# A WKV recurrence rewritten as one phase: token shift inside the projections' weights, four exponents from one difference, the inverse by logarithm and a Newton step

## The chip, the cores and the metric

The kernel runs on one core of a Trainium2 chip. TensorE (PE in the profile) multiplies matrices, VectorE (DVE), ScalarE (ACT) and GpSimd (POOL) work on elements, and each engine runs its own instruction stream in order and meets the others at semaphores. The metric is the device time in microseconds of the whole program; lower is better.

## The reference

The program is a model of several layers over 2 sequences of 1024 tokens with 128 channels: attention, mixtures of experts, and one RWKV layer. The change touches the RWKV layer alone, which computes:

```
xx = concatenate([zeros_like(x[:, :1]), x[:, :-1]], axis=1)
xk = x * time_mix_k + xx * (1.0 - time_mix_k)      # the same for v and r
k, v, r = xk @ W_key.T, xv @ W_value.T, xr @ W_receptance.T
w = -exp(time_decay)
def step(carry, kv_t):                             # over tokens
    p, q, o = carry
    no = maximum(o, u + kt)
    A, Bc = exp(o - no), exp(u + kt - no)
    y = (A * p + Bc * vt) / (A * q + Bc)
    no2 = maximum(w + o, kt)
    A2, B2 = exp(w + o - no2), exp(kt - no2)
    return ((A2 * p + B2 * vt, A2 * q + B2, no2), y)
out = (sigmoid(r) * wkv) @ W_output.T
```

Here `x` is the layer-normed input, `u` is `time_first`, and the output is added to the residual.

## The kernel before

The program is a row of phases. `phase` gives each engine its own block of code, and ends with a barrier of all engines that also clears the phase's semaphores, so nothing of the next phase starts before the last engine of this one is done. Inside a phase `Chain.link` marks an instruction with a semaphore and makes the engine wait for it; `Chain.mark` only marks it.

`rwkv` keeps data with the 128 channels on the partitions and tokens along the free dimension, so one instruction on a sequence is 128x1024. It is called once in `program`, between two calls of `block_l1`. Its pieces in order:

1. `passage` adds the previous block's output to the residual, normalizes, transposes on TensorE and lets ScalarE write the normed input to `rw_x` (line 315). `rw_x` has 1025 columns per sequence, a zero and then the tokens, so the shifted input is the same buffer one column earlier.
2. A phase for constants (lines 1640 to 1653): zeros and start values, `1 - time_mix`, and `-exp(time_decay)` in `rw_w`.
3. A phase for the token shift (1656 to 1667): ScalarE scales `rw_x` by `time_mix` for k, v and r (128x2048 each), and VectorE adds the shifted input scaled by `1 - time_mix`.
4. `products`, a phase of 12 matmuls 128x512 (line 171). Two engines take turns in copying the results from PSUM, VectorE (line 191) and ScalarE (line 200); r passes a sigmoid there.
5. The recurrence's phase (1672 to 1726). VectorE finds `o` by a scan over tokens with add and max (line 1692), forms `no` and the arguments of A, Bc and A2 (1695 to 1698), GpSimd forms B2's (1677), ScalarE takes four exponents for each sequence (1726). Then VectorE scans `q` and `p` (1705, 1707), forms numerator and denominator (1708 to 1712) with GpSimd's product of Bc and v (1680), takes the reciprocal (1713), and multiplies by it and by the gate (1714, 1715). Sequence 0 runs through all of this before sequence 1 starts its second half.
6. `enter_l1`, a `passage` whose first matmuls (line 258) project the result.

The order on each engine is that of the code; there is no scheduler. An fp32 matmul shows as two records of MATMUL in the trace, so the 12 matmuls of step 4 are 24 records. A switch between functions of ScalarE for which the build needs another table puts an ACT_TABLE_LOAD ahead of the activation.

Of the kernel before, what the change touches and what calls it, by code (L numbers as in the profile page):

```python
# [1627 lines left out]
def rwkv(S, D):  # L1628
    with ExitStack() as ctx:
# [10 lines left out]
        with phase(S, 2) as (block, (done, to_act)):  # L1640
            @block.vector
            def _(dve):
                dve.memset(Xs[:, :, 0:1], 0.0)
# [7 lines left out]
            @block.scalar
            def _(act):
                act.activation(wdec[:], S.tdecay[:], ACT.Exp).then_inc(to_act, 1)

        mixes = (mix, A, Bc)
        with phase(S, 1) as (block, (scaled,)):
            @block.scalar
            def _(act):
                for i in range(3):
# [2 lines left out]
            @block.vector
            def _(dve):
                for i in range(3):
                    dve.wait_ge(scaled, i + 1)
                    out = split_b(mixes[i])
                    dve.scalar_tensor_tensor(out, Xs[:, :, 0:T], om[:, i:i + 1], out, ALU.mult, ALU.add)
# [202 lines left out]
```

## Time and profile before

| | |
|---|---|
| time, median of 3 runs (lowest to highest) | 2785.84 us (2783.7 to 2789.19) |
| profiled execution: its time, its span | 2787.93 us, 2786.2 us |
| granted TensorE clock, mean over the span | 0.882 |
| busy: PE, DVE, ACT, POOL | 80%, 57%, 52%, 29% |
| stretch from the end of the first `passage` to the first matmul of `enter_l1` | 2188.7 to 2278.3 us, 89.6 us |
| in that stretch busy: PE, DVE, ACT, POOL | 12.85, 70.91, 22.60, 11.64 us |

The page's shares are over the whole span, in which the RWKV layer is a small part. The stretch of interest is cut out by its times, and its rows are read in order of time. Times in the trace count from the start of the span; the 1.7 us between span and time lie outside of it.

### The profile page before, as it was taken

What the parts mean: (1) busy time and instruction counts of PE and PEld (TensorE: products, weight loads), DVE (VectorE), ACT (ScalarE), POOL (GpSimd) and SP (SyncE); (2) the same over time, 40 slices, a digit from 0 to 9 for tenths busy, and PEclk for the clock granted to TensorE, in tenths of its full rate; (3) what the DMA queues carried; (4) which work ended last, traced back from release to release, by engine and by line L of the source; (5) the groups of instructions that cost most, each with busy time, mean ns of one, the idle gap of its engine ahead of it and who ended that gap; (6) DMA issues with size and microseconds to landing.
All of it is one profiled execution on the core that took longest, in us unless ns stands there. A gap on an engine that the chain in (4) does not pass through costs nothing. (4 is left out here: it accounts for less than half of the span.)

```text
span 2786.2 us, 37366 instructions
## 1 busy us (share of the span) xinstructions
PE 2224.0 (80%) x13838; PEld 1285.9 (46%) x13838; DVE 1588.6 (57%) x3402; ACT 1437.1 (52%) x2136; POOL 804.1 (29%) x384
## 2 busy tenths in 40 slices
PE   4999999999999718499619485999979425999888
PEld 2656666666666415333315243344347212444357
DVE  4777777776776445411355444777433685777324
ACT  2666676666766351388542243455642312555541
POOL 2677777776776201322001203100000022000000
PEclk8899999999999858699759696899989656999999
DMA  2000000000000130321310312211010002210000
GB/s 71 8 1 1 3 8 1 3 8 1 1 3 1 53 103 1 81 67 35 100 56 1 93 33 56 61 36 36 2 31 1 1 0 70 64 36 19 1 31 16
DMA packets 41660, 82.91 MB, mean 30 GB/s; under 512 B 10744, under 2 KB 18472, under 8 KB 37320
## 3 DMA queue, kind: packets, MB, share of 16 engines
q1 hardware_dynamic: 41480, 80.52, 10.7%
q8 instruction: 112, 1.84, 0.3%
q14 instruction: 68, 0.56, 0.1%
HBM read 66.11 MB, written 13.63 MB: 29 GB/s over the span
## 5 line engine op out<-in xcount | busy, mean ns | idle before, releaser
L685 ACT ACTIVATE probs<-psum_banks 128x1024 f32<-128x1024 f32 (+3 forms) x608 | 474.3, 826 | 367.2 <-PE psum_banks L550 260.0
L1096 POOL TENSOR_SCALAR l0a_rows<-l0a_rows,l0a_rinv 128x1024 f32<-128x1024 f32 x192 | 562.2, 2935 | 253.5 <-DVE l0a_rinv L1074 253.3
L758 DVE TENSOR_REDUCE neg_max<-psum_banks 128x1 f32<-128x512 f32 (+3 forms) x672 | 398.8, 658 | 201.4 <-PE psum_banks L583 149.7
L1062 DVE TENSOR_REDUCE l0a_nmax<-psum_banks 128x1 f32<-128x1024 f32 x256 | 312.9, 1222 | 208.7 <-PE psum_banks L955 208.0
L545 PE MATMUL psum_banks<-q_stack,k_stack 75*128 75x512 bf16 (+7 forms) x1216 | 324.9, 345 | 74.5 <-ACT probs L685 25.6
L1009 ACT ACTIVATE l0a_rows<-psum_banks,l0a_nmax 128x1024 f32<-128x1024 f32 x256 | 285.9, 1117 | 81.8 <-DVE l0a_nmax L1062 79.3
L579 PE MATMUL psum_banks<-k_stack,q_stack 72*128 72x128 bf16 (+3 forms) x1024 | 250.3, 328 | 78.1 <-DMA q_stack<-q_parts 66.5
L969 PE MATMUL psum_banks<-packed,l0a_rows 128*128 128x128 f32 x2048 | 267.7, 274 | 7.8 <-POOL l0a_rows L1096 6.3
L954 PE MATMUL psum_banks<-l0a_kh,l0a_qw 128*128 128x512 f32 x512 | 257.4, 503 | 6.1 <-DVE l0a_qw L1030 5.8
L969 PEld LDWEIGHTS psum_banks<-packed,l0a_rows 128*128 128x128 f32 x2048 | 237.9, 141 | 52.5 <-POOL l0a_rows L1096 11.5
L567 PE MATMUL psum_banks<-probs,v_ones 128*32 128x512 f32 (+3 forms) x2432 | 245.8, 520 | 7.5 <-ACT o_sum L654 6.5
L545 PEld LDWEIGHTS psum_banks<-q_stack,k_stack 75*128 75x128 bf16 (+1 forms) x1216 | 106.5, 101 | 254.6 <-ACT probs L685 104.5
L955 PE MATMUL psum_banks<-l0a_kl,l0a_qw 128*128 128x512 f32 x512 | 205.8, 402 | 0.0
L579 PEld LDWEIGHTS psum_banks<-k_stack,q_stack 72*128 72x128 bf16 x1024 | 95.3, 105 | 201.8 <-DVE neg_max L758 90.3
L954 PEld LDWEIGHTS psum_banks<-l0a_kh,l0a_qw 128*128 128x128 f32 x512 | 97.8, 191 | 134.6 <-issue 79.0
L1004 ACT ACTIVATE x_norm<-psum_banks 128x512 f32<-128x512 f32 x128 | 75.9, 593 | 136.8 <-PE psum_banks L969 136.7
L1677 POOL TENSOR_TENSOR rw_b<-rw_k,rw_o 128x1024 f32<-128x1024 f32 x2 | 4.0, 1998 | 459.2 <-DVE rw_o L1692 459.2
L550 PE MATMUL psum_banks<-tri_k,ident_b 128*128 128x128 bf16 (+1 forms) x576 | 133.8, 249 | 0.0
L1623 DVE SCALAR_TENSOR_TENSOR l1f_y<-psum_banks,rt_g,l1f_y 128x128 f32<-128x128 f32 x256 | 72.1, 344 | 103.5 <-PE psum_banks L1561 103.5
L1585 ACT ACTIVATE l1f_h<-psum_banks 128x512 f32<-128x512 f32 x128 | 75.7, 599 | 105.5 <-PE psum_banks L1547 105.2
L981 PE MATMUL psum_banks<-x_norm,l0a_v 128*64 128x512 f32 x512 | 124.0, 604 | 3.7 <-ACT l0a_ot L1014 3.7
L1547 PE MATMUL psum_banks<-x_norm_t,l1f_w 128*128 128x512 f32 x256 | 115.7, 610 | 12.4 <-DMA l1f_w<-in_l1f_w 10.8
(270 smaller groups left out, 3420.9 us busy)
## 6 DMA issues: line engine op xcount, KB each, us to landing
q_stack<-q_parts SPq DMA_DIRECT2D x96, 192.0 KB
k_stack<-k_parts SPq DMA_DIRECT2D x72, 192.0 KB
qkv<-in_l0f_w SPq DMA_DIRECT2D x6, 1024.0 KB, 5.3
q_parts<-parts SPq DMA_DIRECT2D x24, 256.0 KB
k_parts<-parts SPq DMA_DIRECT2D x24, 256.0 KB
moe_b<-in_l0f_b SPq DMA_DIRECT2D x32, 128.0 KB, 4.7
l1f_w<-in_l1f_w SPq DMA_DIRECT2D x16, 256.0 KB, 4.9
moe_w<-in_l0f_w SPq DMA_DIRECT2D x2, 1024.0 KB, 5.5
```

The lines of the kernel that those rows point to most:

```text
L545: m = pe.matmul(PS[:, bank, c0:HALF], S.Kst[0:rows_of_stack, slot(g, i), kt * P:(kt + 1) * P], S.Qst[0:rows_of_stack, slot(g, i), side * H ...
L550: m = pe.matmul(PS[:, bank, c0:c1], S.ident_b[:], S.tri_k[:, 0:c1 - c0], start=False, stop=True, skip_group_check=True)
L567: m = pe.matmul(PS[32 * i:32 * (i + 1), 7, c0:HALF], S.Vx[:, NT * b + kt, h0 + i, :], S.Pt[:, U % PBUFS, i, c0:HALF], start=kt == 0, stop= ...
L579: return pe.matmul(bank[:, at:at + k1 - k0], S.Qst[0:72, slot(g, i), jq * P:(jq + 1) * P], S.Kst[0:72, slot(g, i), k0:k1], start=first, st ...
L685: act.activation(S.Pt[:, U % PBUFS, 2 * half:2 * half + 2, c0:HALF], PS[:, bank:bank + 2, c0:HALF], ACT.Exp).then_inc(exp_done, 1)
L758: dve.tensor_reduce(out, scores, AX, ALU.max, negate=True).then_inc(job_read, 1)
L954: pe.matmul(scores(s)[:, c0:c0 + HALF], q, R.Kh[:, b, c0:c0 + HALF], start=True, stop=False)
L955: m = pe.matmul(scores(s)[:, c0:c0 + HALF], q, R.Kl[:, b, c0:c0 + HALF], start=False, stop=True)
L969: m = pe.transpose(PS[:, 4 + a, jj * P:(jj + 1) * P], R.Pr[:, (NT * ps + 2 * jj + a) % RING, kt * P:(kt + 1) * P], S.ident[:])
L1009: act.activation(R.Pr[:, s % RING, :], scores(s), ACT.Exp, bias=R.nmax4[:, s % 4:s % 4 + 1], accum_out=R.rsum4[:, s % 4:s % 4 + 1]).then_i ...
L1062: dve.tensor_reduce(R.nmax4[:, s % 4:s % 4 + 1], scores(s), AX, ALU.max, negate=True).then_inc(max_done, 1)
L1096: pool.tensor_scalar(R.Pr[:, s % RING, :], R.Pr[:, s % RING, :], R.rinv4[:, s % 4:s % 4 + 1], None, ALU.mult).then_inc(pool_normed, 1)
```

## The change

The phases 2 to 5 become one phase with 14 semaphores.

- The shift goes into the weights. For each of k, v and r two scaled copies of the weight are made (`rw_scaled`, 128x128 each): weight times `time_mix` and weight times `1 - time_mix`. Each bank of 512 tokens is the sum of two matmuls, on `rw_x` and on `rw_x` one column earlier. These are 24 matmuls in place of 12.
- k, v and r stay in PSUM: banks 0 to 3 hold k and later r, banks 4 to 7 hold v. The copies of lines 191 and 200 are gone, VectorE reads k and v from PSUM, and ScalarE reads r for the sigmoid.
- With Z = k - o(previous), all four exponents are `exp(-relu(...))` of Z or -Z with a bias for each channel. VectorE does one scan and one subtraction for a sequence; ScalarE does four Relu and four Exp.
- The reciprocal (1713) is replaced by Ln, Exp of the negative on ScalarE, and a Newton step of three instructions on VectorE that also multiplies the numerator in. GpSimd does nothing in this phase: its subtraction (1677) is gone with the arguments, and its product of Bc and v (1680) moves to VectorE.
- Both sequences' second halves run before either one's division.

```diff
-        mix = S.sb("rw_mix", [P, N])
-        K, V, R = (S.sb(f"rw_{x}", [P, N]) for x in "kvr")
...
+        Z, A, Bc, A2, B2 = (S.sb(f"rw_{x}", [P, B, T]) for x in ("z", "a", "bc", "a2", "b2"))
+        num, den, inv, gate, out = (S.sb(f"rw_{x}", [P, B, T]) for x in ("num", "den", "inv", "gate", "out"))
+        scaled, rest = S.sb("rw_scaled", [P, 3, 2, P]), S.sb("rw_rest", [P, 3])
+        decay, neg_decay, neg_first = (S.sb(f"rw_{x}", [P, 1]) for x in ("decay", "neg_decay", "neg_first"))
...
+        def banks(first, b):
+            return S.PS[:, first + 2 * b:first + 2 * b + 2, :].rearrange("p a c -> p (a c)")
...
+        with phase(S, 14) as (block, (dve_done, act_done, primed, decayed, k_scaled, vr_scaled, k_ready, v_ready, r_ready, z_ready,
+                                      exp_out, den_ready, inverse, gated)):
...
+                def project(i, first, b):
+                    for n in range(T // HALF):
+                        for j in range(2):
+                            t0 = n * HALF + 1 - j
+                            m = pe.matmul(S.PS[:, first + 2 * b + n, :], scaled[:, i, j, :], Xs[:, b, t0:t0 + HALF],
+                                          start=j == 0, stop=j == 1)
+                    return m
+
+                pe.wait_ge(primed, 1)
+                pe.wait_ge(k_scaled, 2)
+                for b in range(B):
+                    project(0, 0, b).then_inc(k_ready, 1)
+                pe.wait_ge(vr_scaled, 4)
+                for b in range(B):
+                    project(1, 4, b).then_inc(v_ready, 1)
+                for b in range(B):
+                    pe.wait_ge(z_ready, b + 1)
+                    project(2, 0, b).then_inc(r_ready, 1)
...
+                ch.link(dve.tensor_scalar(rest[:], S.tmix[:], -1.0, 1.0, ALU.mult, ALU.add))
+                for j, share in enumerate((S.tmix, rest)):
+                    dve.tensor_scalar(scaled[:, 0, j, :], weights[0], share[:, 0:1], None, ALU.mult).then_inc(k_scaled, 1)
...
+                dve.memset(Xs[:, :, 0:1], 0.0).then_inc(primed, 1)
+                dve.wait_ge(primed, 1)
+                dve.wait_ge(decayed, 1)
+                for b in range(B):
+                    dve.wait_ge(k_ready, b + 1)
+                    ch.link(dve.tensor_tensor_scan(O[:, b, cur], decay[:].to_broadcast([P, T]), banks(0, b), -1e38, ALU.add, ALU.max))
+                    dve.tensor_tensor(Z[:, b], banks(0, b), O[:, b, prev], ALU.subtract).then_inc(z_ready, 1)
+                for b in range(B):
+                    dve.wait_ge(exp_out, 4 * b + 2)
+                    ch.mark(dve.tensor_tensor_scan(Qn[:, b, cur], A2[:, b], B2[:, b], 0.0, ALU.mult, ALU.add))
+                    dve.wait_ge(v_ready, b + 1)
+                    ch.link(dve.tensor_tensor(B2[:, b], B2[:, b], banks(4, b), ALU.mult))
+                    dve.wait_ge(exp_out, 4 * b + 4)
+                    ch.link(dve.tensor_tensor(den[:, b], Qn[:, b, prev], A[:, b], ALU.mult))
+                    dve.tensor_tensor(den[:, b], den[:, b], Bc[:, b], ALU.add).then_inc(den_ready, 1)
+                    ch.mark(dve.tensor_tensor(Z[:, b], Bc[:, b], banks(4, b), ALU.mult))
+                    ch.link(dve.tensor_tensor_scan(Pn[:, b, cur], A2[:, b], B2[:, b], 0.0, ALU.mult, ALU.add))
+                    ch.link(dve.tensor_tensor(num[:, b], Pn[:, b, prev], A[:, b], ALU.mult))
+                    ch.mark(dve.tensor_tensor(num[:, b], num[:, b], Z[:, b], ALU.add))
+                for b in range(B):
+                    dve.wait_ge(inverse, b + 1)
+                    dve.wait_ge(den_ready, b + 1)
+                    ch.link(dve.tensor_tensor(B2[:, b], den[:, b], inv[:, b], ALU.mult))
+                    ch.link(dve.scalar_tensor_tensor(inv[:, b], B2[:, b], 2.0, inv[:, b], ALU.subtract, ALU.mult))
+                    ch.link(dve.scalar_tensor_tensor(num[:, b], num[:, b], -1.0, inv[:, b], ALU.mult, ALU.mult))
+                    dve.wait_ge(gated, b + 1)
+                    dve.tensor_tensor(out[:, b], num[:, b], gate[:, b], ALU.mult)
...
-                    act.activation(split_b(mixes[i]), Xs[:, :, 1:T1], ACT.Copy, scale=S.tmix[:, i:i + 1]).then_inc(scaled, 1)
...
+                a = Chain(act, act_done)
+                a.link(act.activation(neg_decay[:], S.tdecay[:], ACT.Exp))
+                act.activation(decay[:], neg_decay[:], ACT.Copy, scale=-1.0).then_inc(decayed, 1)
+                a.mark(act.activation(neg_first[:], S.tfirst[:], ACT.Copy, scale=-1.0))
+                act.wait_ge(dve_done, 1)
+                for i in (1, 2):
+                    for j, share in enumerate((S.tmix, rest)):
+                        act.activation(scaled[:, i, j, :], weights[i], ACT.Copy, scale=share[:, i:i + 1]).then_inc(vr_scaled, 1)
...
+                    act.wait_ge(z_ready, b + 1)
+                    four = (A2, 1.0, neg_decay[:]), (B2, -1.0, decay[:]), (A, 1.0, S.tfirst[:]), (Bc, -1.0, neg_first[:])
+                    for x, sign, bias in four:
+                        a.mark(act.activation(x[:, b], Z[:, b], ACT.Relu, bias=bias, scale=sign))
+                    a.wait()
+                    for x, _, _ in four:
+                        act.activation(x[:, b], x[:, b], ACT.Exp, scale=-1.0).then_inc(exp_out, 1)
...
+                    act.wait_ge(den_ready, b + 1)
+                    a.link(act.activation(inv[:, b], den[:, b], ACT.Ln))
+                    act.activation(inv[:, b], inv[:, b], ACT.Exp, scale=-1.0).then_inc(inverse, 1)
+                    if b == 0:
+                        for c in range(B):
+                            act.wait_ge(r_ready, c + 1)
+                            act.activation(gate[:, c], banks(0, c), ACT.Sigmoid).then_inc(gated, 1)
...
-                for b in range(B):
-                    pool.wait_ge(scanned, b + 1)
-                    pool.tensor_tensor(split_b(B2)[:, b, :], split_b(K)[:, b, :], O[:, b, 1:T1], ALU.subtract).then_inc(b2_in, 1)
...
-                    ch.link(dve.reciprocal(a2, a2))
-                    ch.link(dve.tensor_tensor(k, k, a2, ALU.mult))
-                    ch.link(dve.tensor_tensor(k, k, r, ALU.mult))
```

The instructions of one sequence on VectorE, between exponents and gate. Before, from the scan of `rw_qn` to the product with the gate `rw_r` (`SCALAR_TENSOR_TENSOR` at lines 1705 and 1707 is the scan; buffer numbers are left out, so `rw_a` is A or A2 and `rw_b` is B2):

```order
L1705 SCALAR_TENSOR_TENSOR rw_qn<-rw_a,rw_b 128x1024
L1706 TENSOR_TENSOR rw_k<-rw_b,rw_v 128x1024
L1707 SCALAR_TENSOR_TENSOR rw_pn<-rw_a,rw_k 128x1024
L1708 TENSOR_TENSOR rw_k<-rw_pn,rw_a 128x1024
L1709 TENSOR_TENSOR rw_a<-rw_qn,rw_a 128x1024
L1711 TENSOR_TENSOR rw_k<-rw_k,rw_x 128x1024
L1712 TENSOR_TENSOR rw_a<-rw_a,rw_bc 128x1024
L1713 RECIPROCAL rw_a<-rw_a 128x1024
L1714 TENSOR_TENSOR rw_k<-rw_k,rw_a 128x1024
L1715 TENSOR_TENSOR rw_k<-rw_k,rw_r 128x1024
```

Of the change, the second sequence's part at the same place and the first sequence's division right behind it:

```order
L1689 SCALAR_TENSOR_TENSOR rw_qn<-rw_a,rw_b 128x1024
L1691 TENSOR_TENSOR rw_b<-rw_b,psum_banks 128x1024
L1693 TENSOR_TENSOR rw_den<-rw_qn,rw_a 128x1024
L1694 TENSOR_TENSOR rw_den<-rw_den,rw_bc 128x1024
L1695 TENSOR_TENSOR rw_z<-rw_bc,psum_banks 128x1024
L1696 SCALAR_TENSOR_TENSOR rw_pn<-rw_a,rw_b 128x1024
L1697 TENSOR_TENSOR rw_num<-rw_pn,rw_a 128x1024
L1698 TENSOR_TENSOR rw_num<-rw_num,rw_z 128x1024
L1702 TENSOR_TENSOR rw_b<-rw_den,rw_inv 128x1024
L1703 SCALAR_TENSOR_TENSOR rw_inv<-rw_b,rw_inv 128x1024
L1704 SCALAR_TENSOR_TENSOR rw_num<-rw_num,rw_inv 128x1024
L1706 TENSOR_TENSOR rw_out<-rw_num,rw_gate 128x1024
```

Ten instructions for a sequence become twelve; the reciprocal is gone, and one product with v came from GpSimd (`rw_z`).

ScalarE at the end of the phase. Before, the last rows of the phase are the sigmoids of step 4 and the exponents:

```order
L200 ACT_TABLE_LOAD
L200 ACTIVATE rw_r<-psum_banks 128x512 x4
L66 UNCONDITIONAL_BRANCH
L1717 UNCONDITIONAL_BRANCH
L1726 ACT_TABLE_LOAD
L1726 ACTIVATE rw_a<-rw_a 128x1024
```

Of the change, from the last exponent of the second sequence to the last inverse:

```order
L1727 ACTIVATE rw_bc<-rw_bc 128x1024
L1730 ACT_TABLE_LOAD
L1730 ACTIVATE rw_inv<-rw_den 128x1024
L1731 ACT_TABLE_LOAD
L1731 ACTIVATE rw_inv<-rw_inv 128x1024
L1735 ACT_TABLE_LOAD
L1735 ACTIVATE rw_gate<-psum_banks 128x1024 x2
L1730 ACT_TABLE_LOAD
L1730 ACTIVATE rw_inv<-rw_den 128x1024
L1731 ACT_TABLE_LOAD
L1731 ACTIVATE rw_inv<-rw_inv 128x1024
```

The sigmoids moved from in front of the exponents to between the two sequences' inverses, and five table loads stand in this tail.

## Rows read from the trace of the kernel before

**Rows 1.** Page, part 1: busy time and share of each engine.

```profile
PE 2224.0 (80%) x13838; PEld 1285.9 (46%) x13838; DVE 1588.6 (57%) x3402; ACT 1437.1 (52%) x2136; POOL 804.1 (29%) x384
```

**Rows 2.** Windows: length, busy PE, PEld, DVE, ACT, POOL, granted clock, DMA.

```profile
2188.70:2278.30 89.60, 12.85 (x24) 5.40 (x24) 70.91 (x43) 22.60 (x25) 11.64 (x4) 0.56 0.00 0
2188.70:2201.70 13.00, 0.00 (x0) 0.00 (x0) 7.29 (x9) 7.29 (x6) 0.00 (x0) 0.50 0.00 1
...
2236.00:2278.30 42.30, 0.00 (x0) 0.00 (x0) 40.93 (x21) 2.01 (x3) 4.36 (x1) 0.50 0.00 0
```

**Rows 3.** Timeline, from the passage's end to the last projection.

```profile
2188.11 0.60 ACT L315 ACTIVATE rw_x<-psum_banks 128x512 f32<-128x512 f32 x1 [0.64 <-PE psum_banks L268]
...
2189.82 0.06 DVE L1643 MEMSET rw_x<- 128x2 f32 x1 [2.98 <-PEq L69]
...
2201.73 5.98 PE L171 MATMUL psum_banks<-rw_mix,packed 128*128 128x512 f32 x8 [13.66 <-PEq L69]
...
2203.81 0.69 DVE L191 COPY rw_k<-psum_banks 128x512 f32<-128x512 f32 x1 [2.79 <-PE psum_banks L171]
...
2207.55 3.60 PE L171 MATMUL psum_banks<-rw_a,packed 128*128 128x512 f32 x8
...
2207.75 0.60 ACT L200 ACTIVATE rw_k<-psum_banks 128x512 f32<-128x512 f32 x1 [1.64 <-PE psum_banks L171]
```

**Rows 4.** Windows again: the granted clock (third number from the end).

```profile
2180.00:2190.00 10.00, 3.36 (x13) 2.15 (x12) 6.75 (x38) 2.83 (x7) 0.00 (x0) 0.50 0.00 0
...
2201.00:2206.00 5.00, 4.27 (x5) 1.85 (x6) 0.72 (x2) 0.48 (x1) 0.00 (x0) 0.50 0.01 2
...
2208.00:2212.00 4.00, 4.00 (x11) 1.85 (x10) 1.39 (x2) 1.74 (x4) 0.00 (x0) 1.00 0.00 0
```

**Rows 5.** Timeline of the recurrence: first scan, second half, end.

```profile
2215.93 2.29 DVE L1692 TENSOR_TENSOR_SCAN rw_o<-rw_w,rw_k 128x1024 f32<-128x1024 f32 x1 [4.91 <-PEq L69]
...
2222.56 1.28 DVE L1697 SCALAR_TENSOR_TENSOR rw_bc<-rw_k,packed,rw_mix 128x1024 f32<-128x1024 f32 x1
2222.68 1.06 ACT L1726 ACTIVATE rw_a<-rw_a 128x1024 f32<-128x1024 f32 x1 [5.50 <-DVE rw_a L1696]
...
2235.99 2.28 DVE L1705 TENSOR_TENSOR_SCAN rw_qn<-rw_a,rw_b 128x1024 f32<-128x1024 f32 x1
2236.04 4.36 POOL L1680 TENSOR_TENSOR rw_x<-rw_v,rw_bc 128x1024 f32<-128x1024 f32 x1 [3.45 <-ACT rw_bc L1726]
...
2238.19 3.29 DVE L1706 TENSOR_TENSOR rw_k<-rw_b,rw_v 128x1024 f32<-128x1024 f32 x1
...
2259.95 1.20 DVE L1706 TENSOR_TENSOR rw_k<-rw_b,rw_v 128x1024 f32<-128x1024 f32 x1
...
2268.30 6.55 DVE L1713 RECIPROCAL rw_a<-rw_a 128x1024 f32<-128x1024 f32 x1
2274.89 1.23 DVE L1714 TENSOR_TENSOR rw_k<-rw_k,rw_a 128x1024 f32<-128x1024 f32 x1
2276.15 1.23 DVE L1715 TENSOR_TENSOR rw_k<-rw_k,rw_r 128x1024 f32<-128x1024 f32 x1
...
2278.33 4.42 PE L258 MATMUL psum_banks<-packed,rw_k 128*128 128x128 f32 x24 [63.75 <-PEq L69]
```

**Rows 6.** Groups by line, whole span: count, busy us, mean ns.

```profile
L1018 ACT ACTIVATE l0a_rows<-l0a_rows,l0a_rinv 128x1024 f32<-128x1024 f32 x64 | 73.2, 1143 | 0.0
...
L354 DVE TENSOR_SCALAR x_norm<-l1f_y,ln_mv,ln_rstd 128x128 f32<-128x128 f32 x32 | 8.9, 343 | 0.3
```

**Rows 7.** Timeline of ScalarE around a switch of table, 2211 to 2216 us.

```profile
2211.18 0.60 ACT L200 ACTIVATE rw_v<-psum_banks 128x512 f32<-128x512 f32 x1 [1.12 <-PE psum_banks L171]
...
2211.80 1.28 ACT L200 ACT_TABLE_LOAD   x1
...
2213.09 2.12 ACT L200 ACTIVATE rw_r<-psum_banks 128x512 f32<-128x512 f32 x4
```

More of the change, by code:

```diff
@@ new lines, in rwkv @@
+        num, den, inv, gate, out = (S.sb(f"rw_{x}", [P, B, T]) for x in ("num", "den", "inv", "gate", "out"))
+        scaled, rest = S.sb("rw_scaled", [P, 3, 2, P]), S.sb("rw_rest", [P, 3])
+        decay, neg_decay, neg_first = (S.sb(f"rw_{x}", [P, 1]) for x in ("decay", "neg_decay", "neg_first"))
+        weights = [S.w["rwkv"][x] for x in "kvr"]
+        passage(S, S.X, add=S.Y, to=lambda g: Xs[:, g // 2, 1 + g % 2 * HALF:1 + (g % 2 + 1) * HALF])
+        prev, cur = slice(0, T), slice(1, T1)
@@ L1641, in _ @@
             @block.vector
             def _(dve):
-                dve.memset(Xs[:, :, 0:1], 0.0)
+                ch = Chain(dve, dve_done)
+                ch.link(dve.tensor_scalar(rest[:], S.tmix[:], -1.0, 1.0, ALU.mult, ALU.add))
+                for j, share in enumerate((S.tmix, rest)):
+                    dve.tensor_scalar(scaled[:, 0, j, :], weights[0], share[:, 0:1], None, ALU.mult).then_inc(k_scaled, 1)
                 dve.memset(O[:, :, 0:1], -1e38)
@@ L1646, in _ @@
                 dve.memset(Qn[:, :, 0:1], 0.0)
-                dve.tensor_scalar(om[:], S.tmix[:], -1.0, 1.0, ALU.mult, ALU.add)
-                dve.wait_ge(to_act, 1)
-                dve.tensor_scalar(wdec[:], wdec[:], -1.0, None, ALU.mult)
+                dve.memset(Xs[:, :, 0:1], 0.0).then_inc(primed, 1)
[5 more added lines that the diff above has]
+                    dve.tensor_tensor(Z[:, b], banks(0, b), O[:, b, prev], ALU.subtract).then_inc(z_ready, 1)
@@ L1651, in _ @@
             @block.scalar
             def _(act):
[L1653 to L1659, printed above, removed]
-                    act.activation(split_b(mixes[i]), Xs[:, :, 1:T1], ACT.Copy, scale=S.tmix[:, i:i + 1]).then_inc(scaled, 1)
[L1662 to L1667, printed above, removed]
@@ new lines, in _ @@
+                a.wait()
+                act.wait_ge(decayed, 1)
+                for b in range(B):
+                    act.wait_ge(z_ready, b + 1)
+                    four = (A2, 1.0, neg_decay[:]), (B2, -1.0, decay[:]), (A, 1.0, S.tfirst[:]), (Bc, -1.0, neg_first[:])
+                    for x, sign, bias in four:
+                        a.mark(act.activation(x[:, b], Z[:, b], ACT.Relu, bias=bias, scale=sign))
+                    a.wait()
+                    for x, _, _ in four:
+                        act.activation(x[:, b], x[:, b], ACT.Exp, scale=-1.0).then_inc(exp_out, 1)
@@ new lines, in _ @@
+                for b in range(B):
+                    act.wait_ge(den_ready, b + 1)
[5 more added lines that the diff above has]
+                            act.activation(gate[:, c], banks(0, c), ACT.Sigmoid).then_inc(gated, 1)
+        enter_l1(S, None, token_units(S, S.w["rwkv"]["o"], S.X, src=out.rearrange("p b t -> p (b t)"), add_scale=1.0))
```

54 lines of the change are left out of this document (2 added, 52 removed).

## The prediction

> **What bounds the kernel now.** I read the page's first part only to see that it doesn't decide: over the whole span TensorE is busy 80% and VectorE 57% [rows 1], but the change touches one stretch, and the barriers on both sides of it keep anything from moving in or out. So the second view is the windows of that stretch. From 2188.7 to 2278.3 us VectorE is busy 70.9 of 89.6 us, ScalarE 22.6, TensorE 12.9 [rows 2]. The reader should see two kinds of time in it. In the first 13.0 us TensorE does nothing, while the shift is computed for the whole input before any matmul. In the last 42.3 us VectorE is busy for 40.9 and the others hardly at all [rows 2]. The timeline then gives the borders, and I take four pieces from it:
>
> - head, from VectorE's first memset at 2189.82 to the first projection at 2201.73 [rows 3];
> - projections, from there to the first scan at 2215.93 [rows 3, 5];
> - arguments and exponents, from there to the scan of q at 2235.99, 20.06 us [rows 5];
> - second half, from there to the end of the last product, 2276.15 + 1.23 = 2277.38, 41.39 us [rows 5].
>
> VectorE is the bound in the last two, and the order of phases in the first two. Any microsecond taken off this chain comes off the time, because every later phase starts at a barrier.
>
> **The change on the same clock.** I lay out the new phase from the same first instant, 2189.82. Durations at 128x1024: an operation on two tensors 1.23, a scan 2.29, one with a pointer scalar 1.28 [rows 5]. A linked successor starts 0.03 behind the end (2274.89 + 1.23 to 2276.15); one that doesn't wait overlaps its predecessor by 0.08 (2235.99 + 2.28 against 2238.19) [rows 5]. So linked operations cost 1.26, 1.31 and 2.32 us, unlinked ones 1.15 and 2.20.
>
> *Head.* VectorE makes `rest`, two scaled weights of 0.34 each [rows 6] and four memsets (0.06) [rows 3]. With overlaps that is about 1.0 us, so TensorE starts at 2190.8 instead of 2201.73: **10.9 us** gained. ScalarE meanwhile makes constants and the four scaled weights for v and r; they have until k is projected, some 9 us, and are hidden.
>
> *Projections.* Twice as many matmuls, but only k's first four stand ahead of the first scan. The clock was at 0.50, the 1.2 GHz level, while the passage's short transposes ran (2180 to 2190), still at 0.50 from 2201 to 2206 with TensorE working, and at 1.00, the 2.4 GHz level, from 2208 on [rows 4]. Before, the fourth matmul's result reached ScalarE at 2207.75, 6.02 us behind the start, and the next four (eight records) took 2210.98 - 2207.55, which is 3.43 at full clock (the row's 3.60 holds the last one's overhang) [rows 3]. I assume the same warm-up. k is there at 2196.8 for sequence 0 and 2200.25 for sequence 1; v at 2203.7 and 2207.1; r at 2210.5 and 2214. The first scan starts 6.0 us behind the projections' start instead of 14.2: **8.2 us**. This also removes three barriers. Where no row fits is the scan that reads PSUM. Nothing excludes that it costs as little as a scan from SBUF, 2.29; above, the slowest wide VectorE operation here is the reciprocal with 6.55 [rows 5]. I take 2.29, since a copy of 512 columns from PSUM (0.69 [rows 3]) is far nearer to a scan's pace than to the reciprocal's, and keep 6.55 for the range.
>
> *Arguments and exponents.* Scan 2196.82 to 2199.11, Z until 2200.4. ScalarE then does four Relu with a bias pointer. The nearest row is an activation with a pointer, 1.14, against 1.06 without [rows 5, 6]; successive ones overlap by about 0.1 (four sigmoids of 0.60 take 2.12 [rows 7]). Four Relu 4.3 us, then two exponents 2.0: the scan of q starts at 2206.8, against 9.98 us behind the first scan instead of 20.06: **10.1 us**. Sequence 1's scan and Z (2200.3 to 2203.8) lie in VectorE's wait for these exponents. Here ScalarE, not VectorE, ends the wait: VectorE idles for about 3 us.
>
> *Second half.* For each sequence: scan 2.20, `rw_b` times v 1.26, denominator 1.26 + 1.15, product of Bc and v 1.15, scan 2.32, numerator 1.26 + 1.15 (the 1.15s are those that nothing directly behind waits for). That is 11.75, twice 23.5, to 2230.3. Then the division and gate: 1.26 + 1.31 + 1.31 + 1.15 = 5.03, twice 10.1, ending at 2240.4 or 2240.5. So 33.7 us instead of 41.4: **7.7 us**. Check by parts: two reciprocals (2 x 6.58) go, and the contention of line 1706's first instance, which took 3.29 beside a GpSimd product of 4.36 and 1.20 alone [rows 5], goes with GpSimd: 15.2 less. The division and gate come to 5.03 instead of 2.5 for a sequence, and Bc times v is 1.15: 7.4 more. The difference, 7.8, agrees.
>
> *ScalarE's tail, costed at nothing.* After sequence 1's exponents (about 2216.9): load, Ln, load, Exp for sequence 0 (to 2221.7), load and two gates (to 2224.9), load, Ln, load, Exp for sequence 1 (to 2229.7), with 1.28 for a load and 1.06 for an activation [rows 5, 7]. VectorE asks for the first inverse at 2230.3 and for the second at 2235.4. What hides this work is VectorE's second half; the slack is 8.6 and 5.7 us. Without that cover it would cost all its 12.8 us. TensorE's r is 10 us early for the gates.
>
> *End barrier.* A barrier clears the phase's semaphores. Behind the passage (15) it took 1.1 us (2188.11 + 0.60 to 2189.82) [rows 3], behind the recurrence (6) 0.95 (2277.38 to 2278.33) [rows 5]. With 14 I add 0.15.
>
> Sum: 10.9 + 8.2 + 10.1 + 7.7 - 0.15 = 36.75, I say **36.8 us**. On the profiled execution's own time, 2787.93, that is 2751.1, with a span of 2749.4; that execution lay 2.1 us above the median of the runs, inside their spread. Against the median 2785.84 it is **2749 us**.
>
> **A rule weighed against a row.** When ScalarE switched tables at 2211.8, the load began 0.02 us behind the last activation's end and the sigmoid began 1.29 us later [rows 7]; so I price a switch at 1.29. The Trainium skill (ScalarE: Activation LUTs, section What ACT_TABLE_LOAD costs) puts a drain of 1.38 us on top, 2.66 in all. By it the five switches of the tail would cost 6.9 us more, the second inverse would come at 2236.5 and be 1.1 us late, and the sum would be 35.7 instead of 36.8. The trace speaks against the rule as far as a visible gap goes.
>
> **The rivals.**
>
> 1. *TensorE stays at 1.2 GHz through the phase.* For it: 0.50 over the whole passage and up to 2206 [rows 4]. Against: it rose within some 5 us of steady work. Then k comes 1.2 and 4.6 us later, v at 2211.7 and 2218.5, r at 2225.4 and 2232.2; VectorE waits for v, and the second inverse, behind both gates on ScalarE, comes at 2238. End at 2243.2, 2.7 later: 2751.7.
> 2. *TensorE is at 2.4 GHz at once,* as it idles only 2.7 us before. The first four matmuls take 3.8 instead of 6.0: 2746.8. Against it: 0.50 with intermittent work directly before [rows 4].
> 3. *The scan from PSUM goes at the reciprocal's pace,* 6.55. Both first scans grow by 4.3, of which 5.9 show once the wait for the exponents has taken its share: 2754.9.
> 4. *ScalarE's tail becomes the bound.* If each of the five switches took twice its row, 6.4 us more, the second inverse would be 0.7 late: 2749.7. It decides from 1.15 a switch. Beside it stands the skill's rule above, with 2750.1.
> 5. *The other side, slower: wide VectorE operations contend with ScalarE as they did with GpSimd.* Line 1706 took 3.29 us beside GpSimd and 1.20 alone [rows 5]. The new phase keeps both engines on SBUF and PSUM at once for most of its length. At 3.25 instead of 1.23 for each of the 22 wide operations that are no scans the loss is 44.4, more than the gain by 7.6: 2793. It decides from 19 of the 22. Against it: line 1697, from 2222.56, ran in 1.28 while ScalarE took an exponent from 2222.68, and the scan of 2235.99 wasn't stretched even beside GpSimd (2.28) [rows 5].
> 6. *The change saves here and the rest gives it back,* through a lower granted clock in the 508 us behind it. Nothing in the rows does that; it would end within 0.2%.
>
> **How the numbers follow.** Forecast 0.76; rivals 0.07, 0.05, 0.04, 0.04, 0.02, 0.02 in that order. The likeliest gives 2749. Single runs before lay 2.1 below to 3.4 above their median. The range starts about 3.5 below rival 2 and ends 2 above rival 3: 2743 to 2757. A measurement of this kernel tells about 0.2%, 5.6 us, from no change. All cases but the last two are faster by 31 to 39 us: faster 0.97, same 0.01, slower 0.02 (of rival 6 half is counted as same, half, where only a part is given back, as faster).
>
> **What would show it.** In the changed profile: first projection 1.0 us behind the first VectorE instruction; first scan some 6 us later, in 2.3 us; four Relu of 1.14 and Exps of 1.06 ahead of the scan of q; VectorE without a gap over 0.1 us from there to the end, 33.7 us; no wait for `rw_inv` or `rw_gate`; the stretch 52.8 us instead of 89.6; what lies ahead and behind within a microsecond or two of before. Wrong if the PSUM-reading operations are longer than their SBUF kin, if VectorE's rows are stretched beside ScalarE, if a wait for an inverse shows, or if the 508 us behind change their length.

## The result and the profile after

The changed kernel takes 2750.12 us (median of 4 runs, 2749.71 to 2750.74), beside 2787.52 us before (4 runs, 2783.7 to 2789.27). The ratio is 0.9868, with a 95% interval of 0.9851 to 0.9885: 37.4 us less in the medians, where 36.8 us and a time of 2749 us were forecast.

The timeline of VectorE in the changed kernel, from the constants to the first matmul of `enter_l1` (which stands in TensorE's own timeline, last row; columns as in [rows 3]):

```profile
2186.57 0.17 DVE L1674 TENSOR_SCALAR rw_rest<-packed 128x3 f32<-128x3 f32 x1 [2.94 <-PEq L69]
...
2193.88 2.29 DVE L1685 TENSOR_TENSOR_SCAN rw_o<-rw_decay,psum_banks 128x1024 f32<-128x1024 f32 x1 [6.58 <-PE psum_banks L1656]
2196.20 1.22 DVE L1686 TENSOR_TENSOR rw_z<-psum_banks,rw_o 128x1024 f32<-128x1024 f32 x1
...
2203.88 2.29 DVE L1689 TENSOR_TENSOR_SCAN rw_qn<-rw_a,rw_b 128x1024 f32<-128x1024 f32 x1 [3.00 <-ACT rw_b L1727]
2206.09 1.19 DVE L1691 TENSOR_TENSOR rw_b<-rw_b,psum_banks 128x1024 f32<-128x1024 f32 x1
...
2227.26 1.22 DVE L1702 TENSOR_TENSOR rw_b<-rw_den,rw_inv 128x1024 f32<-128x1024 f32 x1
2228.51 1.22 DVE L1703 SCALAR_TENSOR_TENSOR rw_inv<-rw_b,rw_inv 128x1024 f32<-128x1024 f32 x1
...
2232.17 1.22 DVE L1702 TENSOR_TENSOR rw_b<-rw_den,rw_inv 128x1024 f32<-128x1024 f32 x1
...
2235.94 1.23 DVE L1706 TENSOR_TENSOR rw_out<-rw_num,rw_gate 128x1024 f32<-128x1024 f32 x1
```

```profile
2187.41 23.50 PE L1656 MATMUL psum_banks<-rw_x,rw_scaled 128*128 128x512 f32 x48 [2.55 <-DVE rw_x L1680]
2237.94 5.46 PE L258 MATMUL psum_banks<-packed,rw_out 128*128 128x128 f32 x24 [27.03 <-PEq L69]
```

Inside the phase only two rows of VectorE carry a wait: 6.58 us for k, and 3.00 us for the exponent of B2 (the 2.94 us of the first row are the barrier behind the passage). Behind 2203.88 there is none up to the last product, where the kernel before had its reciprocals and a product of 3.29 us [rows 5].

I call the distance from VectorE's first instruction behind the passage to the first matmul of line 258 the stretch: 88.51 us before (2189.82 to 2278.33 [rows 3, 5]), 51.37 us now (2186.57 to 2237.94), 37.14 less. (The prediction's 52.8 us count from the end of the passage's last row instead, 2184.90 + 0.60 in the changed kernel; by that count it is 52.44.) By the prediction's pieces:

| piece | before | forecast | measured | gain |
|---|---|---|---|---|
| head, to the first projection | 11.91 | 1.0 | 0.84 | 11.07 |
| projections, to the first scan | 14.20 | 6.0 | 6.47 | 7.73 |
| arguments and exponents, to the scan of q | 20.06 | 9.98 | 10.00 | 10.06 |
| second half, to the end of the last product | 41.39 | 33.7 | 33.29 | 8.10 |
| barrier, to the next matmul | 0.95 | 1.10 | 0.77 | 0.18 |

ScalarE's tail in the changed kernel's timeline:

```profile
2212.78 1.04 ACT L1727 ACTIVATE rw_bc<-rw_bc 128x1024 f32<-128x1024 f32 x1
2213.84 1.28 ACT L1730 ACT_TABLE_LOAD   x1
2215.14 1.06 ACT L1730 ACTIVATE rw_inv<-rw_den 128x1024 f32<-128x1024 f32 x1
2216.21 1.28 ACT L1731 ACT_TABLE_LOAD   x1
2217.50 1.06 ACT L1731 ACTIVATE rw_inv<-rw_inv 128x1024 f32<-128x1024 f32 x1
2218.58 1.28 ACT L1735 ACT_TABLE_LOAD   x1
2219.87 1.94 ACT L1735 ACTIVATE rw_gate<-psum_banks 128x1024 f32<-128x1024 f32 x2
2221.83 1.28 ACT L1730 ACT_TABLE_LOAD   x1
...
2225.49 1.06 ACT L1731 ACTIVATE rw_inv<-rw_inv 128x1024 f32<-128x1024 f32 x1
```

The first inverse is there at 2218.56 and asked for at 2227.26, the second at 2226.55 and asked for at 2232.17. Each of the five switches takes 1.30 to 1.32 us from the end of one activation to the start of the next.

The span fell by 38.0 us (2786.2 to 2748.2), 0.9 more than the stretch. Ahead of the stretch the changed execution is 3.25 us shorter (2189.82 against 2186.57), behind it 2.39 longer (507.87 against 510.26), with the same code on both sides. Such differences come in every run below. The part behind the stretch took 506.15 us in e2_old_args and 513.75 in e6_div_at_once, with the same 2873 matmul records. The windows of that part in these two, columns as in [rows 2]:

```profile
2248.25:2754.40 506.15, 423.55 (x2873) 233.45 (x2873) 277.28 (x721) 230.13 (x319) 30.75 (x24) 0.90 0.13 33
```

```profile
2246.05:2759.80 513.75, 431.26 (x2873) 235.63 (x2873) 277.32 (x721) 230.31 (x319) 30.74 (x24) 0.88 0.13 32
```

TensorE is busy 7.7 us longer in the second, at a granted clock of 0.88 instead of 0.90, while VectorE's busy time is the same. So the whole time can't tell edits of 2 or 3 us apart here, and the experiments are read by the stretch first.

### The profile page after: what moved, and what is told of

Its sections match the earlier page's. It is cut to its first block and busy times, and to the rows that moved or that the text cites. A ratio compares the mean times of both kernels' runs of the same rounds, so it can differ in the third digit from the quotient of the medians.

```text
span 2748.2 us, 37340 instructions
## 1 busy us (share of the span) xinstructions
PE 2231.7 (81%) x13852; PEld 1292.2 (47%) x13862; DVE 1558.0 (57%) x3394; ACT 1445.4 (53%) x2148; POOL 792.4 (29%) x380
## 5 line engine op out<-in xcount | busy, mean ns | idle before, releaser
L371 POOL TENSOR_SCALAR l1f_y<-x_res,ln_mv,ln_rstd 128x128 f32<-128x128 f32 x32 | 25.9, 819 | 569.3 <-DVE ln_rstd L351 569.3
L550 PE MATMUL psum_banks<-tri_k,ident_b 128*128 128x128 bf16 (+1 forms) x566 | 127.5, 243 | 0.0
```

Of the source, the lines that this page charges most:

```text
L550: m = pe.matmul(PS[:, bank, c0:c1], S.ident_b[:], S.tri_k[:, 0:c1 - c0], start=False, stop=True, skip_group_check=True)
```

## The experiments

The kernel before, run beside them, took 2786.03 us (19 runs, first four experiments), 2782.17 (7 runs, next four) and 2784.29 (9 runs, last four). My theory: the gain is the sum of four things taken off VectorE's chain, each worth what its rows say, and ScalarE's longer tail costs nothing while VectorE's second half covers it. The main rival: the work has only moved, and ScalarE or TensorE is waited for in its place.

**e1_recip: the reciprocal again.**

```diff
-                    dve.wait_ge(inverse, b + 1)
...
-                    ch.link(dve.tensor_tensor(B2[:, b], den[:, b], inv[:, b], ALU.mult))
-                    ch.link(dve.scalar_tensor_tensor(inv[:, b], B2[:, b], 2.0, inv[:, b], ALU.subtract, ALU.mult))
-                    ch.link(dve.scalar_tensor_tensor(num[:, b], num[:, b], -1.0, inv[:, b], ALU.mult, ALU.mult))
+                    ch.link(dve.reciprocal(inv[:, b], den[:, b]))
+                    ch.link(dve.tensor_tensor(num[:, b], num[:, b], inv[:, b], ALU.mult))
```

> The changed kernel with VectorE's reciprocal in place of Ln, Exp and the Newton step; ScalarE keeps only the two gates in its tail. Stretch here and below: from VectorE's first instruction behind the passage to the first matmul of line 258, 88.5 us before and 51.4 changed. Theory (the inverse by logarithm is worth what it takes off VectorE): a sequence's end goes from 4.91 to 6.58 + 1.26 + 1.15 = 8.99 us, so 8.1 more in all: stretch 59.5, time 8 us over the changed kernel's 2750.1, 2758. Rival (ScalarE's tail is waited for anyway, so the division is no net gain): stretch within 1 us of 51.4.

Measured: stretch 59.59 us (2190.20 to 2249.79), 8.2 more than the changed kernel's; time 2760.52 us, 10.4 more than its 2750.12. From e1_recip's timeline, the end of one sequence:

```profile
2230.97 6.55 DVE L1701 RECIPROCAL rw_inv<-rw_den 128x1024 f32<-128x1024 f32 x1
2237.55 1.23 DVE L1702 TENSOR_TENSOR rw_num<-rw_num,rw_inv 128x1024 f32<-128x1024 f32 x1
2238.81 1.22 DVE L1704 TENSOR_TENSOR rw_out<-rw_num,rw_gate 128x1024 f32<-128x1024 f32 x1
2239.95 6.54 DVE L1701 RECIPROCAL rw_inv<-rw_den 128x1024 f32<-128x1024 f32 x1
```

8.98 us from reciprocal to reciprocal where the change takes 4.91 (2227.26 to 2232.17). The logarithm's route is worth 8.2 us, all of it through ScalarE doing its part in VectorE's shadow.

**e2_old_args: the four arguments on VectorE again.**

```diff
-                    dve.tensor_tensor(Z[:, b], banks(0, b), O[:, b, prev], ALU.subtract).then_inc(z_ready, 1)
+                    dve.scalar_tensor_tensor(A2[:, b], O[:, b, prev], decay[:], O[:, b, cur], ALU.add, ALU.subtract).then_inc(inverse, 1)
+                    dve.tensor_tensor(B2[:, b], banks(0, b), O[:, b, cur], ALU.subtract).then_inc(inverse, 1)
+                    ch.link(dve.scalar_tensor_tensor(num[:, b], banks(0, b), u, O[:, b, prev], ALU.add, ALU.max))
...
-                        a.mark(act.activation(x[:, b], Z[:, b], ACT.Relu, bias=bias, scale=sign))
```

> The changed kernel with the four arguments formed on VectorE as in the kernel before (five instructions behind each scan in place of one) and no Relu on ScalarE. Theory (VectorE's arguments are the chain and there is nothing that they could hide behind but the 3.0 us wait): per sequence 8.3 us from scan to scan instead of 3.5; the scan of q starts 16.6 us behind the first scan instead of 10.0, stretch 51.4 + 6.6 = 58.0, time 2757. The wait of 3.0 us for the exponents is gone. Rival (the work is only moved to ScalarE, whose four Relu are waited for just as long): stretch 51 to 53.

Measured: stretch 56.85 us, 5.5 more; time 2759.03 us, 8.9 more. From the first scan (2197.60) to the scan of q (2214.20) it is 16.6 us, as expected, without a wait. The stretch is 1.1 us less than expected because k came 5.36 us behind the first projection instead of 6.47; that varies from run to run (below). At the changed kernel's 6.47 it would be 57.96.

**e3_shift_alone: the kernel before with the shift in the weights.**

```diff
-                    dve.scalar_tensor_tensor(out, Xs[:, :, 0:T], om[:, i:i + 1], out, ALU.mult, ALU.add)
...
+        products(S, [Unit([(slice(0, HALF), [(scaled[:, i, j, :], Xs[:, n // 2, n % 2 * HALF + 1 - j:(n % 2 + 1) * HALF + 1 - j])
+                                             for j in range(2)])],
+                          dst[:, n * HALF:(n + 1) * HALF], func=ACT.Sigmoid if i == 2 else None)
+                     for i, dst in enumerate((K, V, R)) for n in range(N // HALF)])
```

> The kernel before with one part alone: the shift inside the weights, as 24 matmuls in place of 12 within the old phase of projections, all ahead of the recurrence. Theory (this part pays only because in the changed kernel just four matmuls stand ahead of the first scan): TensorE starts 2.3 us behind VectorE's first instruction instead of 11.9, 9.5 less, and its phase is 24 records of 0.43 longer, 10.3 more: stretch 88.5 + 0.8 = 89.3, no change in time that can be told. Rival (saving the elementwise shift is the gain of head and projections): stretch about 79, time 9 us less than before.

Measured: stretch 88.91 us (2190.44 to 2279.35), 0.4 longer; time 2788.55 us, ratio to before 1.0012 (1.0003 to 1.0022). TensorE started 2.33 us behind VectorE's first instruction, and its 48 records took 22.8 us. The rival is out: saving the elementwise shift, without a change of the order, gains nothing. What is left for the 18.8 us that head and projections gained is the order: only k's first four matmuls stand in front of the first scan, no barrier stands between, and nothing is copied out of PSUM. No run takes these apart, and none has the new order with the elementwise shift. Rows of the kernel before tell what that would cost:

```profile
2192.11 2.00 ACT L1660 ACTIVATE rw_mix<-rw_x,packed 128x2048 f32<-128x2048 f32 x1 [0.87 <-PEq L69]
...
2194.15 2.35 DVE L1667 SCALAR_TENSOR_TENSOR rw_mix<-rw_x,rw_om,rw_mix 128x2048 f32<-128x2048 f32 x1 [2.72 <-ACT rw_mix L1660]
...
2205.52 0.60 ACT L200 ACTIVATE rw_k<-psum_banks 128x512 f32<-128x512 f32 x1 [7.62 <-PE psum_banks L171]
```

Mixing k alone takes 4.4 us (2192.11 to 2196.50), and its first two matmuls 3.8 (2201.73 to 2205.52): 8.2 us to the first scan, where the changed kernel needs 7.3 (2186.57 to 2193.88). By this estimate the shift in the weights would be worth only about 1 us of the 18.8, if VectorE's additions for v and r (2.35 us each) fit into its waits.

**e4_no_pool: the kernel before without GpSimd in the recurrence.**

```diff
-                    pool.tensor_tensor(Xs[:, b, 0:T], split_b(V)[:, b, :], split_b(Bc)[:, b, :], ALU.mult).then_inc(weighted, 1)
...
+                    dve.tensor_tensor(b2, k, O[:, b, cur], ALU.subtract).then_inc(b2_in, 1)
...
+                    ch.link(dve.tensor_tensor(Xs[:, b, 0:T], v, bc, ALU.mult))
```

> The kernel before with GpSimd's four operations in the recurrence done by VectorE. Theory (VectorE's long rows beside GpSimd are contention): lines 1695, 1696 and 1706 all take 1.2 to 1.3 us instead of up to 3.3, which is 7.8 us less, and four more operations of 1.15 are 4.6 more: stretch 85.3, 3.2 less, 0.1% of the time. Rival (they are long for another reason, their operands or the first use of a buffer): the rows stay above 3 us and the stretch grows by 4.6 to 93.1.

Measured: stretch 85.19 us, 3.3 less; time 2787.25 us, ratio 1.0005 (0.9994 to 1.0017), so the whole time doesn't show it. The timelines do. Before, beside GpSimd, three rows of VectorE took 3.1 to 3.3 us besides line 1706's [rows 5]; two of them:

```profile
2218.26 3.12 DVE L1695 SCALAR_TENSOR_TENSOR rw_mix<-rw_k,packed,rw_o 128x1024 f32<-128x1024 f32 x1
...
2230.43 3.25 DVE L1696 TENSOR_TENSOR rw_a<-rw_o,rw_mix 128x1024 f32<-128x1024 f32 x1
```

The same instructions, and line 1706's, in e4_no_pool:

```profile
2215.95 1.28 DVE L1686 SCALAR_TENSOR_TENSOR rw_mix<-rw_k,packed,rw_o 128x1024 f32<-128x1024 f32 x1
...
2225.58 1.22 DVE L1687 TENSOR_TENSOR rw_a<-rw_o,rw_mix 128x1024 f32<-128x1024 f32 x1
...
2232.45 1.20 DVE L1698 TENSOR_TENSOR rw_k<-rw_b,rw_v 128x1024 f32<-128x1024 f32 x1
```

GpSimd made VectorE's four rows longer by 7.8 us (two of 3.12, one of 3.25, one of 3.29) and saved it 4.5. The kernel before shows how [rows 5]: a scan starts at 2235.99, GpSimd's product 0.05 us later and takes 4.36, and VectorE's next product takes 3.29 and ends 1.1 us behind it. The Trainium skill (SBUF — State Buffer, section SBUF: two separate sides) says that VectorE, when it reads two inputs from SBUF, and GpSimd share a port pair, and that whichever starts first holds it for its whole instruction. The trace agrees: 4.36 is near 2.28 for the scan plus the 2.00 that GpSimd's subtraction of the same size takes (line 1677), and the 1.1 us that VectorE's product still needs once GpSimd is done is near the 1.20 that it takes alone.

**e5_pairs: ScalarE does A2 and B2 first.**

```diff
-                    for x, sign, bias in four:
-                        a.mark(act.activation(x[:, b], Z[:, b], ACT.Relu, bias=bias, scale=sign))
-                    a.wait()
...
+                    for two in (four[:2], four[2:]):
+                        for x, sign, bias in two:
+                            a.mark(act.activation(x[:, b], Z[:, b], ACT.Relu, bias=bias, scale=sign))
+                        a.wait()
```

> The changed kernel with ScalarE's order per sequence changed: Relu and Exp of A2 and B2 first, then Relu and Exp of A and Bc. Theory (VectorE's only wait inside the recurrence, 3.0 us for the exponent of B2, holds two Relu that it doesn't need): the scan of q starts two Relu, 2.1 us, earlier, the stretch is 49.4 instead of 51.4 us; A and Bc come 8.3 us behind Z, still ahead of their use. Rival (the wait moves to the second pair, since the denominator needs A and Bc): a new wait of 1 to 2 us in front of line 1693 takes it back, stretch 51.

Measured: stretch 49.00 us, of which 1.1 is an early k (5.39 us). Both sides were right in part. From e5_pairs' waits (who waited for whom, us in total, times, longest):

```profile
DVE rw_qn L1689 <- ACT rw_b L1728: 0.9, 1, 0.9
DVE rw_den L1693 <- ACT rw_bc L1728: 0.8, 1, 0.8
```

The wait of 3.0 us is 0.9 now, and a new one of 0.8 stands in front of the denominator. From first scan to last product it is 41.97 us instead of 43.29: 1.3 gained. The time doesn't show it: 2756.46 us is 6.3 more than the changed kernel's, and 0.9900 of the kernel before run beside it (0.9883 to 0.9917) where the change had 0.9868. The profiled execution spends 513.67 us behind its stretch, the changed kernel's 510.26, with the same code. So the gain is shown for the stretch alone.

**e6_div_at_once: the cover taken away.**

```diff
-                for b in range(B):
                     dve.wait_ge(inverse, b + 1)
```

(the division goes into the loop of the second halves, directly behind each numerator)

> The changed kernel with each sequence's division right behind its numerator, as in the kernel before, so VectorE's second half of sequence 1 no longer covers ScalarE's Ln and Exp of sequence 0. Theory: the first inverse can't be ready before ScalarE has done the exponents of sequence 1 and four pieces of 1.07 to 1.29 us, 14.7 us behind the start of the scan of q; VectorE asks for it 11.7 us behind and waits 3.0; the second one is covered. Stretch 54.4. Rival (all of the tail shows once the cover is gone, as the prediction's 12.8 us would have it): stretch 60 or more. Second rival (no wait at all): 51.4.

Measured: stretch 54.47 us, and one new wait of VectorE in the view of waits:

```profile
DVE rw_b L1701 <- ACT rw_inv L1730: 2.9, 1, 2.9
```

3.1 us longer, not 12.8: what the prediction gave as the price without cover was the length of ScalarE's tail, of which most stays covered. ScalarE begins this tail at 2218.91 and has the first inverse at 2223.64, while VectorE is at its numerator until 2220.73. The second inverse is there at 2237.97 and asked for at 2240.28, so it is covered whole. The time is 2755.49 us, 5.4 more than the changed kernel's, with a wide spread (2749.19 to 2761.50).

**e8_link_end and e7_27_sems: what the last barrier costs.**

```diff
-                    dve.tensor_tensor(out[:, b], num[:, b], gate[:, b], ALU.mult)
+                    ch.link(dve.tensor_tensor(out[:, b], num[:, b], gate[:, b], ALU.mult))
```

> The changed kernel with the last product marked and waited for by VectorE, as the kernel before did. Looked at: the distance from the end of VectorE's last product to the first matmul of line 258, 0.77 us in the changed kernel, 0.95 before. Theory (the old barrier was longer because VectorE waited for its own last instruction, and the number of semaphores to clear plays no part): 0.9 to 0.95. Rival (something else of the old phase, such as its 6 semaphores instead of 14): 0.77 stays.

```diff
-        with phase(S, 14) as (block, (dve_done, act_done, primed, decayed, k_scaled, vr_scaled, k_ready, v_ready, r_ready, z_ready,
-                                      exp_out, den_ready, inverse, gated)):
+        with phase(S, 27) as (block, sems):
```

> The changed kernel with a phase that takes and clears 27 semaphores instead of 14. Looked at: from the end of the last product to the first matmul of line 258, 0.77 us with 14. Theory (the number cleared plays no part): 0.77. Rival (each semaphore costs, as the prediction had it, about 0.02): 1.0.

Measured: with the last product waited for, 1.00 us from its end (2242.74) to the next matmul (2243.74); with 27 semaphores 0.83 (2243.29 to 2244.12). Nine other profiled runs with the unlinked end and 14 semaphores gave 0.77 to 0.80; the three with the old phase (before, e3_shift_alone, e4_no_pool), linked and with 6 semaphores, gave 0.95. So the wait for its own last instruction is what the kernel before paid, 0.2 us, and the number of semaphores costs little: 0.03 to 0.06 for 13 more, 0.05 for 8 more at the linked end. Times: 2753.99 and 2752.52 us, one run each.

**e9_warm: TensorE kept at work through the passage.**

```diff
+            def keep_warm(n):
+                for _ in range(n):
+                    pe.matmul(PS[:, 7, :], S.ident[:], S.iota[:, 0:HALF], start=True, stop=True)
```

> The changed kernel with matmuls 128x512 whose result nobody reads, put into TensorE's gaps in the passage ahead of the recurrence (5 in front of the first transposes, 2, 2 and 1 behind later ones) and one at the start of the new phase. Theory (k's first four matmuls take 6.5 us instead of 3.8 because TensorE comes to them at the 1.2 GHz level after nearly idle 15 us): the granted clock is 1.00 at the first projection, the first scan starts 3.8 to 4.2 us behind it, stretch 51.4 - 2.4 = 49.0. Rival (a level once lost in the passage doesn't come back on such short work, or the extra matmuls at 1.2 GHz delay the transposes): stretch 51.4, and the passage 2 to 5 us longer.

Measured: stretch 48.77 us, k 3.74 us behind the first projection. Windows of the changed kernel (first projection, then on) and of e9_warm (passage, then the first four matmuls); the clock is the third number from the end:

```profile
2187.41:2192.00 4.59, 4.59 (x6) 2.01 (x7) 0.00 (x0) 2.07 (x8) 0.00 (x0) 0.50 0.00 0
2192.00:2196.00 4.00, 4.00 (x10) 1.72 (x9) 2.12 (x1) 0.00 (x0) 0.00 (x0) 0.90 0.00 0
```

```profile
2182.00:2192.00 10.00, 6.87 (x26) 3.24 (x26) 7.73 (x36) 2.58 (x6) 0.00 (x0) 1.00 0.00 0
2193.39:2197.13 3.74, 3.74 (x10) 1.71 (x10) 0.00 (x0) 1.98 (x8) 0.00 (x0) 1.00 0.00 0
```

Without the extra work TensorE is at its 1.2 GHz level (0.50) for the first 4.6 us of the projections, with it at 2.4 GHz (1.00) throughout. The transposes also go faster (0.66 instead of 1.12 us for four), and the passage isn't delayed: from VectorE's first instruction in it to its first behind it, it takes 15.92 us (2176.54 to 2192.46) where the changed kernel takes 16.45 (2170.12 to 2186.57). Stretch and passage together gain 3.1 us. The time of 2748.29 us (2744.68 to 2751.39) is 1.8 less than the changed kernel's, inside the spread.

**f1_best, f4_halves and f2_control: what points further.** f1_best joins e9_warm and e5_pairs and moves one row of VectorE:

```diff
+                    ch.mark(dve.tensor_tensor_scan(Pn[:, b, cur], A2[:, b], B2[:, b], 0.0, ALU.mult, ALU.add))
                     dve.wait_ge(exp_out, 4 * b + 4)
...
-                    ch.link(dve.tensor_tensor_scan(Pn[:, b, cur], A2[:, b], B2[:, b], 0.0, ALU.mult, ALU.add))
```

> The changed kernel with three edits together: TensorE kept at work through the passage, ScalarE's pairs (A2 and B2 first), and the scan of p moved ahead of the denominator, so that A and Bc are asked for 3.4 us later. Theory (the edits' effects add: 2.7 us for k at 2.4 GHz, 2.1 for the pairs, and the 0.8 us wait that the pairs brought is gone): 41.2 us from the first scan to the last product instead of 43.3, stretch 46.7, time 4.5 to 5 us less than the changed kernel measured beside it. Rival (the inverses are late, since the denominator is finished 2.3 us later): a wait of 1 us or more for rw_inv, stretch 47.7 or more.

f4_halves adds to it:

```diff
+                        dve.wait_ge(k_ready, 1)
+                        ch.link(dve.tensor_tensor_scan(O[:, 0, 1:HALF + 1], decay[:].to_broadcast([P, HALF]), S.PS[:, 0, :], -1e38, ALU.add, ALU.max))
+                        dve.wait_ge(k_ready, 2)
+                        ch.link(dve.tensor_tensor_scan(O[:, 0, HALF + 1:T1], decay[:].to_broadcast([P, HALF]), S.PS[:, 1, :], O[:, 0, HALF:HALF + 1], ALU.add, ALU.max))
```

> The former kernel with sequence 0's first scan in two halves of 512 tokens, the first as soon as TensorE has filled its bank. Theory: the first half, 1.2 us, fits in the wait for the second bank, so Z starts 1.1 us earlier and the stretch is 45.6. Rival (a half costs more than half, and the link between the halves eats it): stretch 46.7 or longer.

> The changed kernel, unaltered, beside the others of this call. Its stretch should be 51.4, or 50.3 where TensorE rises to 2.4 GHz one microsecond sooner, as in three of six runs so far; its time tells what the other two are to be compared with, since the 510 us behind the stretch alone have lain between 506 and 514 in runs of unchanged code.

Measured:

| kernel | stretch | time, median (lowest to highest) |
|---|---|---|
| f2_control | 51.60 | 2751.43 (2748.12 to 2754.00) |
| f1_best | 46.36 | 2742.86 (2742.17 to 2743.96) |
| f4_halves | 45.33 | 2746.00 (2743.51 to 2748.05) |

f1_best has no wait left but 0.92 us for B2's exponent and the one for k; its inverses aren't late. It beats the changed kernel run beside it (f2_control) by 8.6 us in the medians, and every run of it is faster than every run of that. The stretch explains 5.2 of it, where 4.5 to 5 were expected; the rest lies in parts with the same code. It is the fastest kernel run, 0.9853 of before (0.9826 to 0.9880). The halves shorten the stretch by 1.0 us more, as expected:

```profile
2189.82 1.22 DVE L1697 TENSOR_TENSOR_SCAN rw_o<-rw_decay,psum_banks 128x512 f32<-128x512 f32 x1 [2.23 <-PE psum_banks L1664]
2191.51 1.28 DVE L1699 TENSOR_TENSOR_SCAN rw_o<-rw_decay,rw_o,psum_banks 128x512 f32<-128x512 f32 x1 [0.47 <-PE psum_banks L1664]
```

but the time doesn't follow: 3.1 us more in the median. In the profiled executions f1_best spends 502.9 us behind its stretch and f4_halves 509.6, with the same code there. TensorE is busy 421.9 us of it in the first, at a granted clock of 0.90, and 428.2 in the second, at 0.89, so the difference again goes with the clock. Whether the halves have any part in it is not settled.

## Why the prediction was right

The time lies 1.1 us from the one forecast, and the mechanism is the forecast one: VectorE's chain got shorter, and nothing was waited for in its place but B2's exponent, 3.0 us, as forecast. That it came so near is partly luck. The terms were off by +0.2, -0.5, 0.0, +0.4 and +0.3 us, which add up to 0.4; k came 1.1 us sooner in half of the profiled runs that started at the same clock; and the code behind the stretch, the same in every run, took 506.2 to 513.8 us in the profiled executions shown above.

- *Head* was right (0.84 for 1.0). Its cause is narrower than the prediction made it: e3_shift_alone gives the head back in the projections (0.4 us longer in all), so head and projections are one term of 18.8 us. That it belongs to the new order is what is left over; it wasn't tested alone.
- *Projections* is the term that was sized least well: 6.47 instead of 6.0. In the eight profiled runs that come to it at 1.2 GHz, k came 5.36 to 5.58 us (four) or 6.47 to 6.70 us (four) behind the first projection; the kernel before's 6.02 lay between. Rival 1 (1.2 GHz throughout) and rival 2 (2.4 GHz at once) didn't occur; e9_warm shows that rival 2's price was right, 3.74 where 3.8 was said.
- *Scan from PSUM* took 2.29 as taken, so rival 3 is out. Products with one operand in PSUM took 1.19 to 1.22, no longer than those from SBUF.
- *Arguments and exponents* were right to 0.02, with Relu at 1.13 to 1.15 and the wait of 3.0; e2_old_args prices the edit at 6.6 us of the 10.06 gained. The other 3.4 are GpSimd's absence, which the prediction had in the sum without naming it: in e4_no_pool this piece takes 16.63 us, against 20.06 before. The prediction read the contention off line 1706 alone; 5.7 of its 7.8 us lay here, in lines 1695 and 1696.
- *Second half* was forecast 0.4 us too long: lines 1703 and 1704 were priced with a pointer scalar (1.28), but their scalars are constants in the instruction and they took 1.22 and 1.23, 0.2 us in all; the rest is hundredths in other rows and rounding. The parts of the 8.1 us gained: e1_recip shows 8.1 for the inverse in this piece (41.42 against 33.29), and e4_no_pool that GpSimd's leaving gave nothing here, 2.1 us of contention against 2.3 for its product on VectorE (41.56 against 41.39).
- *ScalarE's tail at nothing* was right, with slacks of 8.7 and 5.6 us (forecast 8.6 and 5.7). Rival 4 didn't occur: the five switches took 1.30 to 1.32 us. The Trainium skill (ScalarE: Activation LUTs, section What ACT_TABLE_LOAD costs) adds a drain of 1.38 us to each. The trace doesn't agree, and the measurement decides. The price "without that cover, 12.8 us" was wrong, e6_div_at_once gives 3.1.
- *Barrier*: 0.15 us more was forecast, 0.18 less came. The step that failed is that a barrier grows with the semaphores it clears by 0.02 us each; 13 more cost 0.06 at most. Its two rows didn't compare like with like: 1.1 us ran to VectorE's first memset, 0.95 to TensorE's first matmul.
- *Rivals 5 and 6* didn't occur. VectorE's rows kept 1.2 to 1.3 us beside ScalarE, and the part behind the stretch changed by 2.4 us, inside its own spread.

## What to carry to other kernels

A part of a fused change can be worth nothing alone: the shift in the weights saved 9.6 us in front of the matmuls and gave them back in twice as many matmuls, as long as all of them stood in front of the recurrence. So price the order, not the operations removed. GpSimd isn't free help for a VectorE that reads two tensors from SBUF: compare what it takes over (here 4.5 us) with what it stretches (7.8). A slow exact operation on the busy engine can be traded for several on an idle one, as long as other work of the busy engine lies between asking and using; here that meant finishing both sequences' numerators before either division (3.1 us, e6_div_at_once).

## What the runs showed of the hardware

- TensorE's level: idle or on short transposes in the passage it is at 0.50 of its clock [rows 4], and k's first matmuls pay 1.6 to 3.0 us for that in the runs here; matmuls that nobody reads, put into the gaps, hold it at 1.00.
- The same code behind the stretch took 502.9 to 513.8 us in the profiled executions. The two shown above differ in TensorE's granted clock (0.90 and 0.88) and busy time (423.6 and 431.3 us), and not in VectorE's work.
- A scan over 1024 tokens costs 2.29 us from SBUF or PSUM, one over 512 tokens 1.22, and 1.28 with its initial value read from memory, so cutting a scan in two costs about 0.2 us.
